# A two-layer graph kernel on one core: the next pair's one-hots are made one slot earlier, before an evacuation

## The reference, cut to what matters

```
N, D, E = 2500, 1024, 80000          # nodes, features, edges; edges come sorted by dst
h = relu(layernorm(x))
x = x + segment_sum((h @ W0)[src] * edge_weight[:, None], dst)
h = relu(layernorm(x))
deg[i] = 1 + number of edges with dst == i
x = x + segment_sum(norm * (h @ W1.T + b1)[src], dst)     # with self loops,
                                                          # norm = deg^-0.5 of both ends
```

## Time and profile before

| | us |
|---|---|
| median of 3 runs | 1498.34 |
| lowest, highest | 1496.95, 1498.61 |
| the profiled execution | 1499.24 |
| its span, first to last instruction | 1497.5 |
| PE busy | 1447.8 (97%) |
| DVE busy | 955.4 (64%) |
| ACT busy | 441.3 (29%) |
| POOL busy | 289.6 (19%) |

### The profile page before, as it was taken

One profiled execution on the slowest core, in us unless ns is written; L12 is line 12 of the kernel. 1 busy time (PEld: TensorE's weight loads), 2 busy tenths in 40 slices (PEclk: granted clock), 3 DMA queues, 4 the chain that ended last, 5 costly groups with the idle time before them and its releaser, 6 DMA issues.

```text
span 1497.5 us, 24619 instructions
## 1 busy us (share of the span) xinstructions
PE 1447.8 (97%) x7580; PEld 765.4 (51%) x7581; DVE 955.4 (64%) x1728; ACT 441.3 (29%) x869; POOL 289.6 (19%) x576
## 2 busy tenths in 40 slices
PE   3989999999999999999999999999999999999999
PEld 2455555555555554544545444446446446446455
DVE  7789775758777865655655553887555455455542
ACT  7544554422222222322323221823012012011000
POOL 2244332423332322222222220010000000001000
PEclk9999999999999999999999999999999999999999
DMA  8301331337677788788887795913305205204002
GB/s 306 113 24 47 121 101 23 65 74 144 150 160 153 153 179 179 165 175 172 174 179 173 152 191 183 322 54 124 125 1 157 91 1 174 74 14 152 28 1 83
DMA packets 414350, 185.62 MB, mean 124 GB/s; under 512 B 379624, under 2 KB 396540, under 8 KB 414216
## 3 DMA queue, kind: packets, MB, share of 16 engines
q1 hardware_dynamic: 329736, 157.82, 41.8%
q10 hardware_dynamic: 84480, 26.22, 7.1%
HBM read 76.45 MB, written 77.11 MB: 103 GB/s over the span
## 4 chain that ended last, share of the span: by engine, by line
PE 85%; DVE 7%; issue 3%; DMA 2%; ACT 1%; DVEq 1%; SPq 1%; POOL 0%; ACTq 0%; POOLq 0%
PE pair L1746 27%; PE pair L1842 22%; PE pair L1898 13%; PE pair L1630 13%; PE pair L1642 7%; PE pair L1613 1%; PE pair L1699 1%; DVE slots L991 1%; DMA h<-x_scratch 1%; DVE slots L992 1%; DVE slots L988 1%; DVE negbase L1312 1%; DVE slots L986 1%; DMA wstage<-c_scratch 1%; DVEq L1006 0%
## 5 line engine op out<-in xcount | busy, mean ns | idle before, releaser
L1746 PE MATMUL pair<-h,area 128*128 128x512 f16 x2400 | 543.6, 380 | 2.6 <-issue 2.6
L1746 PEld LDWEIGHTS pair<-h,area 128*128 128x128 f16 x2400 | 233.3, 98 | 257.2 <-issue 7.3
L1842 PE MATMUL pair<-area,h 128*128 128x500 f16 x1600 | 339.1, 374 | 1.4 <-DVE h L1246 1.4
L1842 PEld LDWEIGHTS pair<-area,h 128*128 128x128 f16 x1600 | 155.5, 97 | 184.1 <-issue 2.4
L739 POOL TENSOR_TENSOR deg_acc<-deg_acc,area 128x320 f32<-128x320 f32 x160 | 143.2, 895 | 389.0 <-ACT area L1378 389.0
L1898 PE MATMUL pair<-wmat,area 128*125 128x512 f16 x960 | 209.0, 379 | 0.0
L1376 ACT ACTIVATE area<-pair 128x320 f32<-128x320 f32 x160 | 70.0, 438 | 440.8 <-PE pair L1642 434.7
L1898 PEld LDWEIGHTS pair<-wmat,area 128*125 128x125 f16 x960 | 130.6, 136 | 75.5
L1642 PE MATMUL pair<-slots 128*128 128x240 f16 x1120 | 144.0, 266 | 17.9 <-DVE slots L992 17.0
L1051 DVE SCALAR_TENSOR_TENSOR area<-pair,area 128x320 f16<-128x320 f32 x160 | 78.0, 488 | 115.5 <-ACT area L1378 114.5
L1642 PEld LDWEIGHTS pair<-slots 128*128 128x128 f16 x1120 | 108.1, 98 | 66.3 <-DVE slots L992 24.7
(11 more groups left out here) (240 smaller groups left out, 1166.2 us busy)
## 6 DMA issues: line engine op xcount, KB each, us to landing
c_scratch<-area ACTq DMA_DIRECT2D x160, 160.0 KB, 3.0
a_scratch<-area SPq DMA_DIRECT2D x320, 80.0 KB, 2.3
xt<-in_x SPq DMA_DIRECT2D x19, 512.0 KB, 4.0
x_scratch<-xt SPq DMA_DIRECT2D x19, 512.0 KB, 3.6
xt<-x_scratch SPq DMA_DIRECT2D x20, 448.0 KB
out_x<-xt SPq DMA_DIRECT2D x19, 448.0 KB
wstage<-c_scratch SPq DMA_DIRECT2D x17, 500.0 KB, 4.3
slots<-c_scratch SPq DMA_DIRECT2D x17, 500.0 KB, 5.3
```

Source lines behind the costliest of these rows:

```text
L1746: last = pe.matmul(sum_pair(e)[:, half * H:(half + 1) * H], wts(e)[:, q, k, :], hpart(k, r)[:, half * H:(half + 1) * H], start=k == q == r ...
L1842: ins = pe.matmul(sums_of(c, f), hpart(k, q)[:, f * P:(f + 1) * P], counts, start=first and q == 0, stop=last and q == 1, skip_group_check ...
```

## The change

In the later part (`UB`) DVE makes one-hots in odd slots, for the next two quads, ahead of the evacuation. The first pair is made before the loop, in place of a bare wait, so one pair more is made in all; it is not used, and POOL copies fields for it again from the last step. SP waits for it before the counts are loaded, since they land in the same buffer. POOL fetches the fields ahead of the sum of the counts. In `tile`, which the earlier part uses too, the residual goes from slot 1 to slot 2 and the moments from behind `further` in slot 2 to ahead of it in slot 4.

```diff
+        PAST = NQ // 2 + QB // 2 + PRE_STEPS - PQ
...
             sp.wait_ge(win_sum, NQ)
+            sp.wait_ge(hots_ready, PAST + 1)
...
-            def own_step(k, s):
+            def own_step(k, s, of=None):
 
                 pool.wait_ge(hots_ready, k - 1)
-                at = bass.ds((k - PRE_STEPS) * 8, 8)
+                at = bass.ds(((k if of is None else of) - PRE_STEPS) * 8, 8)
...
             with pool.Fori(QB // 4, NQ // 4 - 1) as i:
                 for m in range(2):
                     for s in range(2):
-                        sum_counts(i * 4 + 2 * m + s - 1, 1 - s)
                         if s == 0:
                             own_step(i * 2 + m + 1 + QB // 2 + PRE_STEPS - PQ, 1 - m)
+                        sum_counts(i * 4 + 2 * m + s - 1, 1 - s)
             n = NQ - 4
+            own_step(n // 2 + 1 + QB // 2 + PRE_STEPS - PQ, 1)
             sum_counts(n - 1, 1)
-            own_step(n // 2 + 1 + QB // 2 + PRE_STEPS - PQ, 1)
+            own_step(PAST, 0, PAST - 1)
...
-                    elif q % 2 == 0:
-                        own_hots((td + PRE) * 4 + q // 2 + QB // 2 + PRE_STEPS - PQ, q // 2 % 2, steps_used(n - 2))
+                    elif q % 2 == 1:
+                        own_hots((td + PRE) * 4 + (q + 1) // 2 + QB // 2 + PRE_STEPS - PQ, (q + 1) // 2 % 2,
+                                 steps_used(n - 1))
                     second_part(n - 1, 1 - q % 2)
-                    if q == 1 and not first:
+                    if q == 2 and not first:
                         residual(i - 1 + e, 1 - e)
+                    if q == 4 and not first:
+                        moments_of_x1(i - 1 + e, 1 - e)
                     further(n)
-                    if q == 2 and not first:
-                        moments_of_x1(i - 1 + e, 1 - e)
...
-            dve.wait_ge(step_used, steps_used(QB - 1))
+            own_hots(QB + PRE_STEPS - PQ, 0, steps_used(QB - 1))
             with dve.Fori(ONE_FROM, T // 2 - 1) as i:
```

## The result

| | before | after |
|---|---|---|
| median, us | 1498.47 (4 runs) | 1482.18 (4 runs) |
| lowest, highest | 1496.95, 1500.88 | 1481.45, 1482.84 |
| profiled execution | 1499.24 | 1482.38 |
| its span | 1497.5 | 1480.6 |
| DVE busy | 955.4 | 958.5 |

The changed kernel takes 0.9886 of the time (95% interval 0.9875 to 0.9898; the two medians alone give 0.9891, inside it), 16.3 us less. The forecast was 1483.3 in a range of 1480.0 to 1489.6.

The account below looks back on a forecast made before the run. PE's matmuls plus its standstills, mainly at five turns of DVE's last loop, bound the kernel. Profiled: 1499.24 - 15.2 - 0.5 - 0.5 = 1483.0; taking 15 off the median 1498.34 gave 1483.3, range 1480 to 1489.6.

Parts of the forecast that it names:

- Part 1: Last loop's five turns: one-hots made before DVE's jump back remove PE's waits; 15.2 us won.
- Part 2: Last loop's entry: first one-hots replace a bare wait ahead of it; 0.5 us won, ends 0 and 0.7.
- Part 3: POOL fetches fields ahead of the sum of degrees: worth nothing; were it not moved, 0.5 us of margin left.
- Part 4: Earlier tiles: residual and moments moved to later slots; 0.5 us won, ends 2.4 won and 2.7 lost.
- Part 5: Last slot: one more unused set of one-hots, 1.8 us in DVE's idle time, and SP's wait for it; costs nothing.
- A: Last loop's turns: PE's own jump back, hidden until now, keeps part of each 2.7 us; 1487 to 1497, chance 0.06.
- B: Earlier tiles: residual and moments come wholly on PE's path, giving back 11 us of the gain; 1494, chance 0.06.
- C: Last loop: fields arrive so late that one-hots wait and end after the jump anyway; 1498, chance 0.04.
- E: Last loop: DMA queues don't keep up with iterations of 58.4 us, needing 181 GB/s; counted inside the forecast.
- D: Last loop's turns: jump delays an evacuation freeing PE's buffer; a gap of 11 us gives 1502, chance 0.04.
- the point of 7.6: Last loop's turns: DVE gap in us (4.4 + 3.2) beyond which PE waits for the evacuation after the jump.
- break-even at a gap of 10.3: Last loop's turns: DVE gap in us from which PE loses more than the old 2.7 us a turn.

Follow-up runs that it names:

- the short loop: Kernel before, clamped, old order, with DVE's code for further chunks left out of its last loop (553 rows to 121): 1482.75 us, ratio 0.9888.
- the straight one: Kernel before, clamped, old order, with DVE's last loop of six iterations written out, so no jump there: 1481.88 us, ratio 0.9884.
- the control: Kernel before with only two table-loaded values, waited against, clamped to a range they already keep: 1500.95 us, ratio 1.0014.
- the residual moved alone: Kernel before, clamped, with only the residual moved to slot 2 and the moments to slot 4: 1497.04 us, ratio 0.9986.
- the half turns: Kernel before, clamped, with DVE's last loop as three iterations of four tiles instead of six of two: 1489.58 us, ratio 0.9941.
- the five reductions: Changed kernel, clamped, with five useless 1152-element reductions on DVE just after the last loop's jump: 1511.83 us, ratio 1.0086.
- two reductions added: Changed kernel, clamped, with two useless 1152-element reductions on DVE just after the last loop's jump: 1482.72 us, ratio 0.9889.
- the changed kernel with the clamp: Changed kernel with only two table-loaded values, waited against, clamped to a range they already keep: 1482.20 us, ratio 0.9883.

## Why the prediction was right, point by point

**Part 1**, the turns: 15.2 us foreseen, 15.2 measured (361.7 to 346.5). The whole of it goes, the issue time and the slow products of one turn with it. The gap stays (4.10), now ahead of an evacuation with 3.5 us to spare where 3.2 were worked out. That the gap is the price of the jump rested on one stretch of the chain; the short loop (1482.75) and the straight one (1481.88) show it, both with the old order: it takes a jump and a long body. That it is a fetch of code is inferred.

**Part 2**, the entry: 0.5 won foreseen, 0.1 lost measured. The mis-sized term assumed that one-hots made before the loop would be early. They are just in time: the last of the four ends at 520.8, and PE's products on them begin at 521.08. DVE is still behind from the earlier loop's jump; with that jump gone the entry is two plain slots (7.7 us), in the new order and in the old.

**Part 3**, the fields: nothing, as foreseen; PE doesn't wait without it either, though DVE does, by up to 0.8 us, where a margin of 0.5 was reckoned.

**Part 4**, residual and moments: 0.5 foreseen between +2.4 and -2.7, 0.9 measured, and 1.2 on its own. The prediction said that 1.4 of the 3.8 us lost there was "the turn at 455.73" and that the other 2.4 belonged to the residual and moments. That split fails: with the jump gone and the old order kept, all of it is gone. The residual and moments cost something only where DVE is already behind; moving them wins back about half of the 2.4, removing the jump all of it, paid as it was in instalments. A DVE that is behind meets POOL's sum (a one-hot instruction of 1.15 us).

**Part 5**, the extra one-hots and SP's wait: nothing shows. POOL's sum, though, takes 949 ns in the mean against 895 before (the page's group of `deg_acc`), and POOL's busy time is up by 13.4 us. All of that is hidden.

The terms of parts 2 and 4 missed by 0.6 and 0.4 in opposite directions. The forecast from the profiled execution was 1483.0; it came out at 1482.38. So the terms together gave 16.0 us where 16.2 were foreseen, and the closeness is in part luck: two misses cancel, and another 0.9 us lie outside what the change touches.

**The rivals.** A (a turn of PE's own): refuted, no idle time at any turn; PE's loop is still a hardware loop. B (earlier tiles run out of margin): refuted, they gained. C (fields too late): refuted by the fields left where they were. E (DMA): it does not show, a busy share of 0.84 to 0.86 at 180 GB/s, PE never waiting. D (the evacuation behind the jump becomes the wait): it does not happen, but its place is confirmed. PE's wait appears for a gap of 10.4 and not for one of 7.0, and its size agrees with the point of 7.6. Its price was wrong. The prediction set break-even at a gap of 10.3, and at 10.4 the kernel was 13 us slower than before: the sum left out the granted clock after a standstill, and the experiment added the entry.

## What to carry to other kernels

When an engine's hardware loop shows a gap of the same size at every turn, count the loop's instructions before reordering anything: here DVE's gap was 4 to 5 us a turn with 553 rows, 0.2 with 121, and none in straight code. Moving the work that the others need ahead of the jump hides such a gap; making it unnecessary, by a shorter body or straight code, gives as much, and also in places where there is no slack to hide it in. A delay on an engine with little margin can be paid for many slots after its cause, so look for the first place where the engine falls behind, not at the slots where PE waits.

## What the runs showed that was not expected

- In the last loop the granted clock falls only behind standstills of PE, and not behind all. In that of before, of the control, of the residual moved alone, of the half turns and of the five reductions there are 5 + 5 + 5 + 2 + 6 = 23 standstills; behind 1 + 3 + 0 + 1 + 4 = 9 of them the next 15 products take 4.5 to 6.0 us instead of 3.40, a stretch between the levels of 1.2 and 2.4 GHz. Of the four longest (2.79 to 4.19 us) all have it, of the 19 of 1.65 to 2.67 us five. In the kernels without a standstill there it never happens in the last loop. It fits that the four runs of before spread over 3.9 us and those of after over 1.4. What decides among the shorter ones stays open, and it isn't the length alone: a wait of 1.91 us has it in one trace and not in another, so has one of 1.98, and one of 2.67 has not.
- A wait can carry a false name. As long as a wait for POOL's fields stood first behind the jump, the profile of the kernel before put DVE's gap down to them at four turns of five; it called the same gap "issue" at the fifth, and at all five once an evacuation stood there. The gap at the fifth, 4.87 us, is not in the 18.3 us of the earlier trace rows.
- A wait that grows need not be a loss. With two reductions added ACT waited 39 times for the DMA of `a_scratch`, 109.8 us in all; in the changed kernel with the clamp it was 9 times and 24.2 us. But its waits for PE's products fell from 224.6 to 131.7 us, so ACT stood still as long as before (246 and 249 us in all): only the one that came last had changed.
